# A planned four-layer transformer kernel: scale and shift after the transposition, rows spread by DMA, shorter reflection steps, MLP in halves of 256 rows

## What is computed

```python
mod = silu(c) @ w_ada + b_ada              # six rows of 288 per batch
sh1, sc1, g1, sh2, sc2, g2 = split(mod, 6)
h = ln(x) * (1 + sc1) + sh1
x = x + g1 * (attention(h @ w_qkv + b_qkv) @ w_proj + b_proj)   # 16 heads of 18
h = ln(x) * (1 + sc2) + sh2
x = x + g2 * mlp(h)                        # 288 -> 1152 -> 288, gelu
# layer 0: four experts, all computed for all rows, mixed by the top two gates
# stage 3: U, _ = qr(P);  R = expm(A(silu(c) @ W.T + b)),  P is 288 x 64
z = x @ U;  out = x + (z @ R - z) @ U.T
```

## Time and profile before

| what | value |
|---|---|
| median of 3 runs | 1620.38 us (1617.28 to 1622.78) |
| the profiled execution, its own time | 1614.11 us |
| its span | 1612.3 us, 30341 instructions |
| busy: PE, PEld, DVE, ACT, POOL | 86%, 51%, 62%, 49%, 26% of the span |
| mean granted TensorE clock | 0.940 of full speed |
| DMA | 106.09 MB, mean 66 GB/s |

### The profile page before, as it was taken

The page is one execution under the profiler, slowest core; times in us unless marked ns, Lnnn a source line. Parts: engine busy times, 40 slices in busy tenths (PEclk is TensorE's granted clock), DMA queues, the critical chain, the costliest instruction groups (busy, mean ns, idle before and its releaser), DMA issues.

```text
span 1612.3 us, 30341 instructions
## 1 busy us (share of the span) xinstructions
PE 1391.3 (86%) x11814; PEld 826.6 (51%) x11814; DVE 1004.1 (62%) x2361; ACT 787.7 (49%) x1534; POOL 412.9 (26%) x551
## 2 busy tenths in 40 slices
PE   3667988988899989899898987898998899899977
PEld 1333554544455555555455554464554456565634
DVE  4676766467585666566574766856647687766442
ACT  2553545656475434454343544555444465555522
POOL 1011314133332332233231332323413131231100
PEclk9788989999999999999999999899999899999968
DMA  6232234443122210221212212230011010000010
GB/s 174 63 120 76 75 106 143 138 137 107 62 60 70 84 68 19 71 77 58 80 30 91 57 73 87 56 78 20 27 42 49 28 54 26 24 13 9 27 38 15
DMA packets 80389, 106.09 MB, mean 66 GB/s; under 512 B 39469, under 2 KB 67318, under 8 KB 76918
## 3 DMA queue, kind: packets, MB, share of 16 engines
q1 hardware_dynamic: 78134, 101.79, 20.6%
q10 hardware_dynamic: 2112, 2.36, 0.5%
HBM read 87.37 MB, written 16.49 MB: 64 GB/s over the span
## 4 chain that ended last, share of the span: by engine, by line
PE 51%; DVE 19%; issue 12%; DMA 6%; ACT 5%; POOL 5%; SPq 2%; POOLq 0%; DVEq 0%; ACTq 0%
PE P L1323 21%; DVE NM L1737 4%; PE P L1476 4%; PE P L1477 4%; PE P L1478 4%; PE P L1445 3%; PE P L1436 2%; PE P L1343 2%; DMA QT<-MT 1%; PE P L1412 1%; POOL N L2162 1%; POOL X L2147 1%; PE P L1333 1%; DVE AT L1869 1%; DMA STG<-in_L_b 1%
## 5 line engine op out<-in xcount | busy, mean ns | idle before, releaser
L1323 PE MATMUL P<-XT,W 128*128 128x512 f16 x1512 | 356.3, 387 | 14.4 <-DVE NM L1737 6.2
L2147 POOL TENSOR_TENSOR X<-X,TM 128x288 f32<-128x288 f32 x144 | 121.9, 847 | 716.4 <-DVE TM L1812 480.5
L1476 PE MATMUL P<-W,H 128*128 128x288 f16 x864 | 254.6, 295 | 1.9 <-POOL H L2152 1.8
L1477 PE MATMUL P<-W,H 128*128 128x288 f16 x864 | 254.1, 294 | 0.0
L1478 PE MATMUL P<-W,H 128*128 128x288 f16 x864 | 253.9, 294 | 0.0
L1323 PEld LDWEIGHTS P<-XT,W 128*128 128x128 f16 x1512 | 142.9, 99 | 193.5 <-issue 25.1
L2061 ACT ACTIVATE ARENA<-P 128x512 f32<-128x512 f32 x256 | 137.8, 602 | 131.8 <-PE P L1436 131.4
L2071 ACT ACTIVATE G<-P 128x512 f32<-128x512 f32 x216 | 128.4, 594 | 109.8 <-PE P L1323 99.9
L1737 DVE TENSOR_REDUCE NM<-P 128x2 f16<-128x512 f32 x256 | 160.3, 687 | 1.4 <-PE P L1421 0.5
L2152 POOL TENSOR_TENSOR H<-G,H 128x512 f16<-128x512 f32 x98 | 121.8, 1248 | 133.2 <-ACT H L2072 132.8
L1323 PE MATMUL P<-WQ,XT 128*128 128x288 f16 x1008 | 151.6, 303 | 4.2 <-issue 3.1
(11 more groups left out here) (293 smaller groups left out, 2266.0 us busy)
## 6 DMA issues: line engine op xcount, KB each, us to landing
W<-scr_w SPq DMA_DIRECT2D x9, 1440.0 KB, 6.2
W<-scr_w SPq DMA_DIRECT2D x9, 1368.0 KB, 5.8
ADB<-scr_ada SPq DMA_DIRECT2D x24, 432.0 KB, 3.9
ADB<-scr_ada SPq DMA_DIRECT2D x24, 288.0 KB, 4.8
scr_w<-W SPq DMA_DIRECT2D x4, 1440.0 KB, 5.9
scr_w<-W SPq DMA_DIRECT2D x4, 1368.0 KB, 5.0
STG<-in_L_w SPq DMA_DIRECT2D x10, 432.0 KB, 3.4
STG<-in_L_w SPq DMA_DIRECT2D x7, 576.0 KB, 5.0
```

The costliest lines, as they stand in the source:

```text
L1323: ins = e.matmul(o, l, r, start=k == 0, stop=k == len(pairs_) - 1)
L1476: e.matmul(o, hi, W2[:, 2 * m, :], start=False, stop=False)
L1477: e.matmul(o, hi, W2[:, 2 * m + 1, :], start=False, stop=False)
L2147: e.tensor_tensor(X[:, t, :], X[:, t, :], TM[st["k"]][:, :], ALU.add).then_inc(st.sem)
```

## The change

1. The condition's rows for scale and shift are no longer stored to DRAM and broadcast. `cond_T` transposes each product of the condition on PE and `cond_cols` (ACT) keeps it as columns in SC. Only the two gate rows go through DRAM (`g1_in`, 144 KB for each batch instead of 288 and 432 KB). In `layernorm`, YL is transposed first; `full` (three instructions on ACT or DVE) multiplies by a column and adds a column on the way out of PSUM into FULL; `m_hi` (ACT or DVE) and `m_lo` (DVE or POOL) make XT from FULL. `ln_scale` and `ln_shift` are gone.
2. `t_bc` is replaced by `t_spread`: 16 DMAs from SP, each from one partition of RCP to 32 partitions. `t_norm` then reads SBUF.
3. `householder` is a line of its own of rank 4, ready from the start. The row is broadcast by a DMA from SP (`hh_row`); ACT only squares; POOL does five operations on one column; DVE does four. What the step left undone on the first column is added once at the end (`hh_v`).
4. `up` works on 256 rows at a time: two blocks of the hidden dimension share a bank, 14 matmuls of 256 columns per group (4 such groups and one of 7 per half). `down` waits for the parts of its own half. The last chunk is two passes, each of which can start when its batch is ready (SPLIT).
5. Two planner constants change, SLACK from -0.3 to -0.46 and the planned cost of a matmul, and the products of layer 0's condition go two blocks at a time, those for A three.

```diff
+LANDS = dict(t_spread=3.5, w_back=6.0, w_keep=5.8, g1_in=3.3, ...
+SPLIT = {(2, 3): [(0,), (1,)]}
+SLACK, BIAS = -0.46, 0.2
...
-            s = do(dve, "ln_scale", 0.76, w=w, sc=sc, src=z, rows=rows or ask())
-            lane, cost = sooner([s], (pool, 1.5), (dve, 0.76))
-            r = do(lane, "ln_shift", cost, ..., w=w, sh=sh, src=s)
-            yield from to_columns(b, YL[w], r, mixed)
+            m = do(pe, "xb_T", 0.8, y=YL[w], js=(j, j2), full=z, free=[pf, pf2])
+            f = copy("full", 1.1 + BIAS, 1.15, L=L, b=b, sc=sc, sh=sh, ..., src=m, cols=cols, free=ff)
+            hi = copy("m_hi", 0.95 + BIAS, 0.75, b=b, i=i, src=f, free=before)
+            lane, cost = sooner([hi], (pool, 2.5), (dve, 1.35))
+            lo = do(lane, "m_lo", cost, ..., src=hi, free=before)
...
-                    m = do(pe, "t_bc", 0.55, c=c, i=kr, j=j, src=r, free=jf)
+            bc = do(sp, "t_spread", 0.6, incs=256, i=kr, src=r, free=ef)
...
-                m = do(pe, "hh_mm", mm_cost(1, C - j, 4) + 0.1, c=j, j=c, src=last, free=pf)
-                a = do(act, "hh_row", 0.55, incs=2, c=j, j=c, src=m, free=last if j else None)
-                p = do(pool, "hh_root", 0.67, src=a, half=hp)
-                d = do(dve, "hh_step", 2.3, incs=10, c=j, src=a, root=p, at=p_in)
+                r = do(sp, "hh_row", 0.1, incs=16, c=j, src=last)
+                a = do(act, "hh_norm", 0.5, c=j, src=r)
+                p = do(pool, "hh_root", 2.0, incs=5, c=j, src=a, half=hp, free=last if j else None)
+                d = do(dve, "hh_step", 1.4, incs=4, c=j, src=a, root=p, at=p_in)
...
+                q.wait_ge(st["src"], st["at"], st["root"].at(4), ...)
+                e.tensor_tensor_reduce(out=HQ[:, j:C], in0=bc, in1=aj, ..., accum_out=w)
+                e.reciprocal(rt, TI[:, j:j + 1])
+                e.scalar_tensor_tensor(out=g, in0=w, scalar=rt, in1=NMK[:, j:j + 1], ...)
+                e.scalar_tensor_tensor(out=aj, in0=bc, scalar=g, in1=aj, ...)
...
+            def t_spread(st):
+                for s in range(4):
+                    for c in range(4):
+                        e.dma_start(spread_of(st["i"], c)[32 * s:32 * s + 32, :], RCP[32 * s + c:32 * s + c + 1, :]...)
+            def hh_row(st):
+                e.dma_start(BC[:, c:C], AT[c:c + 1, c:C].unsqueeze(1).broadcast_to([1, D, C - c]))
...
-                products(bank(st), [(W1[...], XT[:, x, c * 512:(c + 1) * 512]) for x, w in PRODUCTS], st)
+                for k, m in enumerate(range(st["m"], min(st["m"] + 2, 9))):
+                    for i, (x, w) in enumerate(PRODUCTS):
+                        ins = e.matmul(bank(st)[:, 256 * k:256 * k + 256], W1[...], XT[:, x, at:at + 256], ...)
```

More of the change, by code:

```diff
@@ L319, in cond_rows @@
                 yield [a]
-                s = do(sp, "cond_out", 0.1, raises=f"os{o}", incs=16 * len(some), o=o, dst=tuple(dst[:, (k + g) * C:(k + g + 1) * C] for g in some), src=a)
-                rOS.free[o] = [s]
-                stores = [x for x in stores if x.sem is not s.sem] + [s]
+                last = []
+                some = [g for g in some if L is None or k + g in (2, 5)]
+                if some:
+                    last.append(do(sp, "cond_out", 0.1, raises=f"os{o}", incs=16 * len(some), o=o, gs=tuple(some), dst=tuple(dst[:, (k + g) * C:(k + g + 1) * C] for g in some), src=a))
+                    stores = [x for x in stores if x.sem is not last[0].sem] + last
+                if L is not None:
+                    yield from slot(rP)
+                    _, j, pf = rP.take()
+                    m = do(pe, "cond_T", 0.4, o=o, n=32 * len(bufs), j=j, src=a, free=pf)
+                    rOS.free[o] = last + [m]
+                    yield [m]
+                    c = do(act, "cond_cols", 0.65, L=L, k=k, n=len(bufs), j=j, src=m)
+                    rP.free[j] = [c]
+                    for g in range(len(bufs)):
+                        tok["cols", L, k + g] = c
+                else:
+                    rOS.free[o] = last
                 for g in some:
@@ L487, in layernorm @@
             yield
-            while (("ada", L), 1) not in tok:
-                yield "wait"
-            s = do(dve, "ln_scale", 0.76, w=w, sc=sc, src=z, rows=rows or ask())
-            yield
-            lane, cost = sooner([s], (pool, 1.5), (dve, 0.76))
-            r = do(lane, "ln_shift", cost, raises=f"ln_shift_{lane.name}", w=w, sh=sh, src=s)
-            yield
-            yield from to_columns(b, YL[w], r, mixed)
-            rYL[w].free[0] = tok["read"]
-            tok["lnd"] = [r]
+            yield from two(rP)
+            _, j, pf = rP.take()
+            _, j2, pf2 = rP.take()
+            m = do(pe, "xb_T", 0.8, y=YL[w], js=(j, j2), full=z, free=[pf, pf2])
+            rYL[w].free[0] = [m]
+            yield [m]
+            while ("cols", L, sc) not in tok or rF.held():
+                yield "wait"
+            _, i, ff = rF.take()
+            cols = [tok["cols", L, sc], tok["cols", L, sh]]
+            before = TR[2 * b] + TR[2 * b + 1]
+            f = copy("full", 1.1 + BIAS, 1.15, L=L, b=b, sc=sc, sh=sh, mixed=mixed, i=i, js=(j, j2), src=m, cols=cols, free=ff)
+            rP.free[j], rP.free[j2] = [f], [f]
+            yield [f]
+            hi = copy("m_hi", 0.95 + BIAS, 0.75, b=b, i=i, src=f, free=before)
+            yield [hi]
+            lane, cost = sooner([hi], (pool, 2.5), (dve, 1.35))
+            lo = do(lane, "m_lo", cost, raises=f"m_lo_{lane.name}", incs=3 if lane is pool else 1, b=b, i=i, src=hi, free=before)
+            rF.free[i] = [lo]
+            for t in (2 * b, 2 * b + 1):
+                TW[t], TR[t] = [xt_ones, hi, lo], []
+            yield
         def prep_tokens(b, u, wr_v, full_q, full_k):
@@ L564, in prep @@
             u = b % 2
-            def ask():
-                return do(sp, "ad_in", 0.1, raises=f"ad{u}", incs=16, u=u, L=L, b=b, free=ad_rd[u], src=tok[("ada", L), 1])
-            rows = ask() if (("ada", L), 1) in tok else None
             yield
-            yield from layernorm(0, L, b, AD1[u][:, C:2 * C], AD1[u][:, 0:C], rows, L == 1, ask)
-            ad_rd[u] = list(tok["lnd"])
+            yield from layernorm(0, L, b, 1, 0, L == 1)
             if L == 2 and b == 0:
@@ L885, in finish @@
                 ot_rd[0] = ms_
-            yield from layernorm(1, L, b, AD2[u][:, 2 * C:3 * C], AD2[u][:, C:2 * C], rows)
-            ae_rd[u] = [tok["lnd"], v]
+            g1_rd[u] = [v]
+            yield from layernorm(1, L, b, 4, 3)
             if L == 0:
@@ L1192, in start @@
                     need = self.change(1)
-                    self.steps, self.side = down(L, e, c), w1_load(*need) if need else iter(())
+                    self.steps, self.side = down(L, e, c, vs), w1_load(*need) if need else iter(())
             def change(self, way):
@@ L1299, in bank, with inner @@
             return P[st["j"]]
+        def inner(st):
+            m, z = st["m"], min(st["m"] + 2, 9)
+            hi, lo = (H[:, st["v"], m:z, k, :] for k in range(2))
+            n = 256 * (z - m)
+            return hi, lo, G32[st["gi"]][:, 0:n], n
         def half(st):
@@ L1393, in t_av @@
                 ins.then_inc(st.sem)
-            def t_bc(st):
-                q.wait_ge(st["src"], st["free"])
-                for s in range(4):
-                    k = 32 * s + st["c"]
-                    ins = e.matmul(bank(st)[32 * s:32 * s + 32, 0:256], IDF[:, k:k + 1].broadcast_to([128, 32]), E1[st["i"]][:, 0, 0:256],
-                                   start=True, stop=True, tile_position=(0, 32 * s))
-                ins.then_inc(st.sem)
             def t_proj(st):
@@ L1866, in hh_step @@
-                q.wait_ge(consts, st.at(6))
-                e.scalar_tensor_tensor(out=g, in0=w, scalar=rt, in1=NMK[:, j:j + 1], op0=ALU.mult, op1=ALU.mult).then_inc(st.sem)
-                q.wait_ge(st.at(7))
+                bc, aj = BC[:, j:C], AT[:, j:C]
+                g, rt, w = (HS[:, k:k + 1] for k in range(3))
+                q.wait_ge(st["src"], st["at"], st["root"].at(4), (st.sem, st.first) if st.first else None)
+                e.tensor_tensor_reduce(out=HQ[:, j:C], in0=bc, in1=aj, scale=1.0, scalar=0.0, op0=ALU.mult, op1=ALU.add, accum_out=w).then_inc(st.sem)
```

405 lines of the change are left out of this document (218 added, 187 removed).

## The result

The changed kernel takes **1630.52 us** (median of 4 runs, 1628.58 to 1631.21) beside 1619.84 for the kernel before (4 runs, 1617.28 to 1622.78): ratio 1.0063, 95% interval 1.0044 to 1.0083. It is 11 us slower, 0.6%, a small loss but clear of the noise, where 1548 us and 72 us less were forecast, and it lies outside the range. The profiled execution's own time is 1631.21 us.

The account below looks back on a forecast made before the run. PE, busy 86% of the span, was taken to bound the kernel. Terms of 111 us off and 39 on gave net 72 off the profiled 1614.1, 1542, and with 6.3 for the median 1548 us (chance 0.52), range 1500 to 1595.

Parts of the forecast that it names:

- Reciprocals in layer 1: Layer 1: dropping `t_bc` saves PE 16 us and 6 of waits; spread DMAs holding DVE cost 20, bounds 0 and 63.
- Rival B: Layer 1's spread: all 63 us reach PE, or those and SP's delay, instead of 20: 1591 us, chance 0.10.
- Rival C: Reflection steps: DVE's wait for POOL, ACT waiting for the row's DMA before it, becomes PE's: 109 us, 1647 us, chance 0.07.
- Reflections: Reflections: 64 matmuls off PE save 39 us, and 25 of waits (bounds 0 and 34); new waits cost PE 10.
- rival E: Reflection matmuls only filled time PE would have waited anyway: 39 and 25 shrink to a third, 1591 us, chance 0.10.
- half the sign: Reflection steps: DVE waits on POOL above 1.5 us, and behind them new PE waits on DVE over 1 us each.
- Halves and tail: MLP: `up` in 256 columns costs 6 us (bounds 0 and 85); the last chunk's two passes save 15 (0 to 21).
- rival D: `up` in the MLP: 256 columns cost 0.136 us each, +79 us, 1627 us, chance 0.04.
- Layernorm: Shorter path before the transposition: saves 5 us in the first stretch, 5 elsewhere, bounds 0 and 20; `cond_T` costs 3.

Follow-up runs that it names:

- e1: The changed kernel with layer 1's reciprocals spread by fp32 matmuls on PE again instead of by DMAs, all else as changed: 1518.44 us, ratio 0.9378.

## Why the prediction was wrong, step by step

**Reciprocals in layer 1: the step that failed.** The mechanism was seen, and its size was not. The step took 0.29 to 0.64 us for an issue from DMAs of another kind, 5 us of hold of DVE a batch, of which half reached PE: 20 us, bound 63. The issues took 0.59 us for the first few and 1.17 for the rest, 15.2 to 16.9 us a set, and they landed 5.5 us after the issue at the median where 2.9 were taken; DVE waited 14 us a batch, 112.4 in all. The spread as a whole costs 112 us net against the matmuls: the 16 us of PE work that it saves, less 128 us of idle time and lower clock. The upper bound was no bound: it was made of the largest median of an issue in the kernel before, though a row there had a maximum of 1232 ns, and no row had one partition as the source of 32 copies.

A second part of that step was left "to the range": SP's queue held 10 us. It was held over 15, a reflection's row stood behind it, ACT behind that row and the maxima row behind ACT (30 of the 36.0 us of PE's waits); and it remains at 1601 us when the plan knows the length.

Rival B was the right one of the five by its mechanism; its price of 63 us is half of the 128. Rival C's second clause, ACT waiting in order for the row's DMA, had its share in it. The page of the Trainium skill that was weighed there (DMA: Bandwidth & Descriptors, where the 2 us go) has its 50 ns of dispatch in the account of a DMA issued from GpSimd, and these go out from SP; by an estimate from it the sixteen would have been dispatched in 0.8 us. The trace does not bear that out for SP: the shortest issue of the line took 512 ns.

**Reflections: half right.** The 39 us of PE's work are there (35 to 43 in three pairs). The 25 us for waits are not: the pairs differ by 53, 23 and 13 us, mean 30, where 39 + 25 - 10 = 54 were forecast, and by -17 at the old constants.

This lies between the forecast and rival E, which leaves 64 / 3 - 10 = 11, though E had the saved work shrink too. E's sign, idle time growing by as much as the work shrinks, came in the changed kernel (78 against 61 us), but by the spread: without it PE was busy 1332 us and idle 186, near the 1345 and 195 forecast. Of rival C half the sign came: DVE waited for POOL in 20 of the 64 steps of the changed kernel, 64.2 us in all, 3.2 each and up to 7.9, where 1.9 were the most forecast. In e1 it waited 79.1 us for POOL, yet PE's largest group of waits on DVE, for the maxima (L1459), is 15.4 us there and was 14.9 before, so this did not become PE's wait at C's price. The chain was to take 440 us and ended at 1080, which is still before its result is wanted.

The step's four operations ran in 1.25 us where 1.4 was forecast, as this timeline of DVE in the changed kernel has them:

```profile
586.90 0.42 DVE L1889 CUSTOM_DVE_ANT_0 HQS<-HQS,AT 64x256 f32<-64x256 f32 x1 [1.90 <-issue]
...
587.25 0.15 DVE L1891 RECIPROCAL HS<-TI 64x1 f32<-64x1 f32 x1
587.44 0.21 DVE L1893 SCALAR_TENSOR_TENSOR HS<-HS,NMK 64x1 f32<-64x1 f32 x1
587.68 0.47 DVE L1895 SCALAR_TENSOR_TENSOR AT<-HQS,HS,AT 64x256 f32<-64x256 f32 x1
```

But the row's landing was taken as 2.9 us from a DMA of another shape and is 4.0 at the median.

**Halves and tail: right beside the new constants.** The `up` matmuls took 359.3 us on PE in the changed kernel, and the halves' cost of 6 us measured 7.5 in one comparison. 256 columns cost half of 512 (15.60 us for 126, 15.66 for 63), so rival D is out. The tail's 15 us measured 10 from the split; the clock of that window, called halved there, was 0.75. With the old constants and reflections the two together gave 22 us, not 9.

**Layernorm: undersized.** 22 us (17 to 34) where net 7 was taken and 20 less 3 was the upper bound, as far as one order can say. I did not find which of its parts does it; DVE's and POOL's busy time both fell in that run (971.8 us against 1004.1, 385.0 against 412.9, so POOL shed 28 and not 48).

**The constants: not priced.** The diff showed them, and the prediction had no term. They are worth 69 us beside the new reflections, nothing beside the old ones and -14 us in the kernel before. In this kernel a changed constant redraws the order of 30,000 instructions.

**The sum.** By the runs, in the order of building up: 22 for the layernorm, 22 for halves and split, nothing for the constants, 53 for the reflections, 97 together, against 98 measured between the kernel before and e1, as it must be when each step starts where the last one ended; then 112 on for the spread. The forecast without the spread's cost and gain was 72 + 20 - 22 = 70 off. So the rest of the change did better than forecast, 98, and one line of it took all back. Of the 28 us above the forecast 23 may be luck: that is by how much the reflections' pair at these constants lies above the mean of the three. The shares of reflections, halves and constants hold for this order of adding them, since they depend on each other. The spread's 112 us hold beside the new reflections, with which it made the longest waits for the maxima row. The spread alone in the kernel before was not tried, nor the change with its old constants.

## What to carry to other kernels

A DMA's issue time belongs to its shape and to what is already under way in its queue: look at the first issues of a set and the later ones apart, as a median mixes them. A broadcast out of one partition is priced from such a broadcast, or left unpriced with a bound that says so; many small DMAs in one queue are a hold of the whole queue, to be charged to everything queued behind. In a kernel whose order is planned, a measured difference of one pair is the edit plus a redraw of the order: vary a neutral constant and compare means before believing 20 us. And an idle PE pays again in its clock.

## What was unexpected of the hardware

A DMA from one SBUF partition to 32, 32 KB, took 591 ns to issue when few were under way and 1168 ns behind them (1058 at the median of all), and 5.5 us to land; with 32 partitions as its source, the same bytes took 591 ns and 1.9 us at the median, and a whole set went out at that pace. One source partition moved 30 GB/s with the DMA engines 0.81 busy, 32 of them 52 GB/s at 0.26. A row of AT to 64 partitions landed in 3.6 us at the least and 4.0 at the median, where a copy of whole partitions had 2.9. And two kernels with the same 13225 matmuls had PE busy for 1331.9 and 1355.6 us, by granted clocks of 0.951 and 0.930.
